# An attention kernel whose work order comes from a written-out table instead of per-beat patterns

## The chip, the cores and the metric

The kernel runs on one core of a Trainium2 chip. The metric is the device time of one execution in microseconds (us), the median of several runs. The program is one launch; every engine runs its own instruction stream, and semaphores order them.

## The reference

Eight images of 32 x 32 tokens with 128 channels pass through four attention layers in a row, all in fp32.

- Layers 0 and 1: group norm, then attention with 8 heads of 16 channels over the 1024 tokens of an image (softmax over 1024 keys), output projection, residual. 
- Layer 2: layer norm over the channels, attention with one head of 128 channels, projection, residual.
- Layer 3: group norm, attention with one head of 128 channels, projection, residual.

```python
def _L0_conv_ref(x, gn_scale, gn_bias, w_qkv, w_out, b_out):
    ...
    scores = jnp.einsum('bcq,bck->bqk', q, k) * hd ** (-0.5)
    scores = jax.nn.softmax(scores, axis=-1)
    o = jnp.einsum('bqk,bck->bqc', scores, v)
...
    x = _L0_conv_ref(x, ...)
    x = _L1_conv_ref(x, ...)
    x = _L2_conv_ref(x, ...)
    x = _L3_conv_ref(x, ...)
    return x
```

## The kernel before

**Work of a layer with heads (0 and 1).** An image and layer make a head stage of four rounds; a round is 4 heads by 512 queries. Per round TensorE makes

- 32 *tiles* (`score_tile`, L1292): scores of 128 queries by 512 keys for one head, contracted over one half of the array's rows (62 of 128); neighbouring tiles use opposite halves. VectorE takes the row maximum of each (L1084). A tile lands in one of `WORK_BANKS` = 3 PSUM banks, and the bank is free when VectorE has read it.
- one *shift* (L1278/L1280): the 16 columns of maxima are turned, split in two parts, and four DMAs put them into rows of `q_stack`, so that the second product of scores comes out with the maximum subtracted.
- 16 *pairs* (`pair`, L1320): scores again, keys by queries, with the shift in the product: two matmuls on opposite row halves into one of two PSUM buffers (`pairs`); ScalarE takes the exponential of 1024 columns (L973).
- 8 times *values* (`values`, L1346): the products of probabilities and values for 4 heads at once, each on 32 columns of the array, over 512 queries in one go (`("values", u, 0, 2)`) or in two halves of 256 (`("values", u, 0, 1)` and `("values", u, 1, 1)`).

So 64 rounds hold 2048 tiles, 1024 pairs and 512 slots; a *slot* is what lies between the values of one key block and those of the next: two pairs, one values, and as many tiles as the plan puts there.

**Work of a layer with one head (2 and 3).** For 128 queries at a time (`full` beats, 128 in all): *scores* (L1364), maximum on VectorE (L1116), exponential on ScalarE (L980), *turn* (eight transposes, L1208) and a copy by ScalarE (L989), and four steps *pv* per 128 queries (L1386). Seven phases of such beats are put between and behind the head stages.

**Chunks.** Everything else is a chunk: transposes of an image (`in`, `up`, `back`), the two group-norm products (`gn1`, `gn2`), the projections (`k0` to `v1`) and the output projections (`out0`, `out1`), of 512 columns each, all on TensorE with a bank of their own; and steps without a bank (`stats`, `apply`, `lnstats0`, `lnapply0` and so on). The text below calls the projections and output projections *products*. Where a product stands next to values it is issued as four matmuls of 32 columns (`by_columns`, L1217), else as one of 128 (L1214).

**What sets the order.** `Plan` writes one list, `plan.order`, when the program is built. Each engine walks the same list and issues its part of every item, so the list fixes the order on every engine and on the SP queue. `place_chunks` gives each chunk a beat. `place_tiles` spreads the tiles over the beats between what is available and what is due, as evenly in time as it can, where a head beat weighs 1.0 and a full beat `FULL_BEAT_WEIGHT` = 1.1. `beat(b)` then orders what a beat holds by a pattern chosen by its number of tiles (T a tile, P a pair, C the chunks of the beat, V values in one go, U one half of values):

```python
    PATTERNS = {0: "PCPV", 1: "TPCPV", 2: "TPCTPV", 3: "TPCTTPV", 4: "TPCTTPTV"}
    SHIFT_LAST = True
    HALVES_PATTERN = "TPTPCUTTV"
    CHUNK_PATTERNS = {0: "PPVC", 1: "TPPVC", 2: "TPTPVC", 3: "TPTPTVC", 4: "TPTCUTPTV"}
```

`count` walks the finished list and gives out banks, ring places and semaphore counts; a chunk in a beat with fewer than four tiles goes to a `work` bank (`narrow`), others to a `pairs` buffer. A wait in the list is thus bound to the item before it that used the same bank.

Of the kernel before, what the change touches and what calls it, by code (L numbers as in the profile page):

```python
# [1 line left out]

# [5 lines left out]
P = 128  # L8
# [16 lines left out]
SLOTS = KT * ROUNDS  # L25
# [32 lines left out]
HALVES = PROJECTIONS + ("out0", "out1")  # L58
# [13 lines left out]
class Plan:  # L72
# [5 lines left out]
    def __init__(self):  # L78
        self.beats, self.head_beat, self.full_beat = [], {}, {}
        n = 0  # L80
        for g in range(len(HEAD_STAGES)):
            for s in range(STAGE_SLOTS):
                self.head_beat[g, s] = len(self.beats)
                self.beats.append(("head", STAGE_SLOTS * g + s))
            for _ in range(KT * FULLS_AFTER.get(g, 0)):
                self.full_beat[n] = len(self.beats)
                self.beats.append(("full", n))
                n += 1
        self.full_tiles = n
# [58 lines left out]
    def place_chunks(self):  # L148
        h, f, put = self.h, self.f, self.put
        one = list(PROJECTIONS)  # L150
        two = ["k0+k1+q0+q1", "v0+v1"]
        ln = ["up", "lnstats0", "lnstats1", "lnapply0", "lnapply1", "back"]
        ln_fast = ["up", "lnstats0+lnstats1", "lnapply0+lnapply1", "back"]
        last = IMAGES - 1
        for i in range(IMAGES):
            g0, g1 = self.head_index[0, i], self.head_index[1, i]
            k2, k3 = self.full_index[2, i], self.full_index[3, i]

            if i == 1:
# [24 lines left out]
            if i < 2:  # L184
                end = self.chain(h(2 * i + 3, 6 if i == 0 else 1), 2, i, ln)
                self.project(end + 1, 2, i, one)
            elif i < last:
                end = self.chain(f(k2 - 1, 1), 2, i, ln_fast)
                self.project(h(2 * i + 3, 1), 2, i, one)
            else:  # L190
                self.project(self.chain(f(k2 - 1, 1), 2, i, ln_fast), 2, i, two)

            up = ["up", *NORM]
            if i < last - 2:
                at = h(6, 13) if i == 0 else h(2 * i + 6, 13)
                self.project(self.chain(at, 3, i, up), 3, i, one)
            elif i == last - 2:
                self.project(self.chain(h(15, 13), 3, i, up), 3, i, one)
            else:
                self.project(self.chain(f(k3 - 1, 1), 3, i, ["up", "stats", "gn1+gn2", "apply"]), 3, i, two)  # L200

    def place_tiles(self):


        ready = [0] * len(HEAD_STAGES)
        for g, b in self.available.items():
            slots = self.STACK_SLOTS
            while slots > 0:
                slots -= 1 if self.beats[b][0] == "head" else 2
                b += 1  # L210
            ready[g] = b
        tiles = [(r, n) for r in range(ROUNDS) for n in range(TILES)]
        ends = len(self.beats)
        time, most, least = [0.0], [self.FIRST_TILES], [self.FIRST_TILES]
        for b, (kind, _) in enumerate(self.beats):
            time.append(time[-1] + (1.0 if kind == "head" else self.FULL_BEAT_WEIGHT))
            most.append(TILES * ROUNDS_OF_STAGE * sum(r <= b for r in ready))
            least.append(0)
        for r in range(1, ROUNDS):
            due, slots = self.head_beat[r // ROUNDS_OF_STAGE, KT * (r % ROUNDS_OF_STAGE)], self.DUE_BEFORE  # L220
            while slots > 0 and due > 0:
                due -= 1
                slots -= 1.0 if self.beats[due][0] == "head" else self.FULL_BEAT_WEIGHT
            for b in range(max(due, ready[r // ROUNDS_OF_STAGE] + 5), ends + 1):
                least[b] = max(least[b], TILES * (r + 1))
        least = [min(low, high) for low, high in zip(least, most)]
        done, at = [float(self.FIRST_TILES)], 0
        while at < ends:
            low, high, low_at, high_at, to = -1.0, 1e9, at, at, at
            while to < ends and low <= high:  # L230
                to += 1
# [1252 lines left out]
```

## Time and profile before

| | |
|---|---|
| time, median of 3 runs | 2267.25 us (2265.59 to 2267.3) |
| span of the profiled execution | 2270.4 us |
| TensorE busy | 2160.2 us, 95% |
| VectorE busy | 1688.7 us, 74% |
| ScalarE busy | 1454.0 us, 64% |
| GpSimd busy | 408.0 us, 18% |
| mean granted TensorE clock | 0.983 |

The profiled execution's span is 2270.4 us, 3.1 us above the median of the runs; the profile's own time and the measured one can be taken as the same to 0.14%. A busy TensorE is not a TensorE at its peak: the end of a matmul in the profile is modelled, and where a matmul stands alone on one half of the array the engine counts as busy too. So the distance between the starts of neighbouring items says more than busy time.

### The profile page before, as it was taken

To read this page: it belongs to the slowest core of one execution; us is meant where nothing else is said; L and a number is where in the kernel's file an instruction comes from. 1 tells how busy PE (TensorE), PEld (TensorE's weight loads), DVE (VectorE), ACT (ScalarE), POOL (GpSimd) and SP (SyncE) were. 2 spreads that over 40 slices of the span, in tenths; PEclk is the share of its full clock that TensorE was granted. 3 is DMA by queue.
4 is the path that set the end of the run, shared out by engine and by line. 5 is a ranking of instruction groups with operands and counts; after the bars stand their busy time and mean duration, and the time that the engine had idled before them with its cause. 6 is when DMAs were issued, how large, how long until landed. Compare 5 with 4: busy or idle time off the path is not lost.

```text
span 2270.4 us, 41605 instructions
## 1 busy us (share of the span) xinstructions
PE 2160.2 (95%) x16748; PEld 1158.8 (51%) x16748; DVE 1688.7 (74%) x3104; ACT 1454.0 (64%) x1698; POOL 408.0 (18%) x541
## 2 busy tenths in 40 slices
PE   5999999999999999999999999999999989999999
PEld 3444344434643467434764347533574335745888
DVE  6899898889688876888668886788767956772433
ACT  1577677767477754778458774587646875476554
POOL 3102111220122311212111221203121030021231
PEclk7899999999999999999999999999999999999999
DMA  5403142230231403031130402204040050000000
GB/s 137 83 14 83 41 76 63 43 83 13 54 51 40 56 23 76 16 72 24 52 62 2 94 2 65 49 2 94 2 94 11 2 94 1 6 6 1 5 6 19
DMA packets 48590, 97.45 MB, mean 43 GB/s; under 512 B 7824, under 2 KB 10640, under 8 KB 48272
## 3 DMA queue, kind: packets, MB, share of 16 engines
q1 hardware_dynamic: 48400, 94.81, 20.1%
q8 instruction: 133, 2.18, 0.4%
q14 instruction: 57, 0.47, 0.1%
HBM read 55.98 MB, written 37.75 MB: 41 GB/s over the span
## 4 chain that ended last, share of the span: by engine, by line
PE 79%; DVE 13%; issue 4%; ACT 2%; POOL 1%; DMA 1%; SPq 0%; POOLq 0%; ACTq 0%; DVEq 0%
PE outs L1346 19%; PE work L1292 19%; PE outs L1386 11%; DVE part_max L1084 8%; PE pairs L1364 8%; PE pairs L1320 8%; PE pairs L1208 5%; PE work L1217 4%; PE pairs L1217 3%; PE work L1214 1%; DVE o_turn L1096 1%; DVE stats L1022 1%; DVE neg_max L1116 1%; ACT probs L973 1%; DMA q_stack<-shift_parts 1%
## 5 line engine op out<-in xcount | busy, mean ns | idle before, releaser
L1084 DVE TENSOR_REDUCE part_max<-work 128x1 f32<-128x512 f32 x2048 | 1284.5, 681 | 236.8 <-PE work L1292 232.2
L973 ACT ACTIVATE probs<-pairs 128x1024 f32<-128x1024 f32 x1024 | 1005.4, 1023 | 313.6 <-PE pairs L1320 298.6
L1292 PE MATMUL work<-k_stack,q_stack 62*128 62x512 f32 x2048 | 743.9, 468 | 31.5 <-DVE part_max L1084 20.7
L1320 PE MATMUL pairs<-q_stack,k_stack 64*128 64x512 f32 x2048 | 611.5, 440 | 13.4 <-DMA q_stack<-shift_parts 10.9
L1346 PE MATMUL outs<-probs,v_heads 128*32 128x256 f32 (+1 forms) x5448 | 584.2, 500 | 7.2 <-DVE o_turn L1096 6.9
L1292 PEld LDWEIGHTS work<-k_stack,q_stack 62*128 62x128 f32 x2048 | 317.2, 187 | 529.4 <-DVE part_max L1084 355.9
L1116 DVE TENSOR_REDUCE neg_max<-pairs 128x1 f32<-128x1024 f32 x128 | 156.6, 1223 | 236.2 <-PE pairs L1364 235.5
L1320 PEld LDWEIGHTS pairs<-q_stack,k_stack 64*128 64x128 f32 x2048 | 271.8, 186 | 57.1 <-ACT probs L973 31.0
L980 ACT ACTIVATE probs<-pairs,neg_max 128x1024 f32<-128x1024 f32 x128 | 142.8, 1115 | 245.9 <-DVE neg_max L1116 245.9
L1386 PE MATMUL outs<-v_full,probs 128*128 128x128 f32 x2048 | 258.6, 279 | 4.8 <-issue 4.8
L1386 PEld LDWEIGHTS outs<-v_full,probs 128*128 128x128 f32 x2048 | 242.5, 192 | 35.8 <-issue 32.1
L1346 PEld LDWEIGHTS outs<-probs,v_heads 128*32 128x32 f32 x5448 | 114.2, 108 | 222.7 <-issue 195.3
L1364 PE MATMUL pairs<-k_full,q_full 128*128 128x512 f32 x768 | 211.8, 411 | 7.2 <-ACT probs L980 2.5
L861 POOL TENSOR_TENSOR o_both<-o_turn,o_inv 128x256 f32<-128x256 f32 x64 | 39.7, 620 | 805.7 <-DVE o_inv L1099 805.6
L989 ACT COPY probs<-pairs 128x1024 f32<-128x1024 f32 x128 | 129.8, 1014 | 54.1 <-PE pairs L1208 54.1
L1364 PEld LDWEIGHTS pairs<-k_full,q_full 128*128 128x128 f32 x768 | 134.8, 188 | 53.9 <-issue 13.0
L1208 PE MATMUL pairs<-avg,probs 128*128 128x128 f32 x1024 | 134.3, 274 | 0.4
L1208 PEld LDWEIGHTS pairs<-avg,probs 128*128 128x128 f32 x1024 | 116.9, 142 | 19.8 <-issue 16.4
L883 POOL CAST parts<-parts 128x512 fp32r<-128x512 f32 x64 | 39.1, 611 | 270.8 <-ACT parts L944 270.5
L819 POOL TENSOR_TENSOR rstd<-var_eps,minus_half 128x1 f32<-128x1 f32 (+1 forms) x32 | 26.7, 834 | 328.5 <-DVE var_eps L1047 249.3
L885 POOL TENSOR_TENSOR parts<-parts 128x512 fp32r<-128x512 f32 x64 | 82.0, 1282 | 5.1
L1217 PE MATMUL work<-h,w 128*32 128x512 f32 x472 | 64.2, 602 | 0.0
(126 smaller groups left out, 1136.6 us busy)
## 6 DMA issues: line engine op xcount, KB each, us to landing
k_scratch<-parts SPq DMA_DIRECT2D x64, 256.0 KB
q_scratch<-parts SPq DMA_DIRECT2D x64, 256.0 KB
k_stack<-k_scratch SPq DMA_DIRECT2D x64, 256.0 KB, 7.0
q_stack<-q_scratch SPq DMA_DIRECT2D x64, 256.0 KB, 9.7
k_stack<-k_scratch SPq DMA_DIRECT2D x64, 128.0 KB, 8.3
q_stack<-q_scratch SPq DMA_DIRECT2D x64, 128.0 KB, 10.7
q_stack<-shift_parts SPq DMA_DIRECT2D x256, 4.0 KB
tmp<-x SPq DMA_DIRECT2D x7, 512.0 KB, 3.5
```

The costliest lines, as they stand in the source:

```text
L973: nc.scalar.activation(probs[:, plan.prob[u], 2 * n:2 * n + 2, :], pairs[:, plan.half["pair", t], :, :], ACT.Exp, scale=HEAD_SCALE).then_i ...
L980: nc.scalar.activation(p_full[:, n % 2, :], bank_of(("scores", n)), ACT.Exp, bias=neg_max1[:, n % SUMS:n % SUMS + 1], accum_out=sum1[:, n ...
L989: nc.scalar.copy(pT_full[m % 2][:, :, P * (n % 2):P * (n % 2 + 1)], bank_of(("turn", n)).rearrange("p (k q) -> p k q", q=P)).then_inc(f_co ...
L1084: nc.vector.tensor_reduce(part_max[:, r % 2, column:column + 1], bank_of(("tile", r, n)), AX_X, ALU.max, negate=True).then_inc(tile_max, 1)
L1116: nc.vector.tensor_reduce(neg_max1[:, n % SUMS:n % SUMS + 1], bank_of(("scores", n)), AX_X, ALU.max, negate=True).then_inc(f_max, 1)
L1208: last = nc.tensor.transpose(bank[:, P * n:P * (n + 1)], source(j), ident)
L1217: last = nc.tensor.matmul(to[some, :], weights[:, some], moving, start=True, stop=True)
L1292: nc.tensor.matmul(bank_of(("tile", r, n)), qs[rows, i, a, heads, P * t:P * (t + 1)], ks[rows, i, keys, heads, :], start=True, stop=True). ...
L1320: last = nc.tensor.matmul(pairs[:, plan.half["pair", t], half, :], ks[rows, i, key // QT, first + n, P * (key % QT):P * (key % QT + 1)], q ...
L1346: last = nc.tensor.matmul(outs[2 * HD * n:2 * HD * (n + 1), columns], v_heads[:, i, key, at:at + 2 * HD], probs[:, plan.prob[u], n, column ...
L1364: last = nc.tensor.matmul(pairs[:, plan.half["scores", n], half, :], q_full[:, k % 2, q, queries], k_full[:, k % 2, key, columns_of(half)] ...
L1386: last = nc.tensor.matmul(outs[:, P * j:P * (j + 1)], pT_full[m % 2][:, k, P * j:P * (j + 1)], v_full[:, at % 2, k, :], start=k == 0, stop ...
```

## The change

Three things change, all in `Plan`; no instruction of an engine is added or changed in kind.

1. The finished order goes through a new function, `arranged`. It takes tiles, pairs and all other items (class C) each from a queue of its own, in their old order, and merges them by a table of letters, `FIRST_STEPS` and `STEPS`. V and U make the values of the next slot, in one go or in halves. The patterns of `beat` still decide the order within class C, and nothing else.
2. The layer norm of the images 2 to 6 in layer 2 goes over six beats (`ln`) and not four (`ln_fast`).
3. In `place_tiles` a head beat with a product weighs 1.2 and not 1.0, so more tiles are given to such a beat. As the table fixes where tiles stand, this touches the place of the shifts among class C, and which products count as `narrow`.

```diff
@@ -100,7 +101,89 @@
             self.order += self.beat(b)
         m = self.full_tiles // 2 - 1
         self.order += self.full_values(2 * m + 1) + [("y", m)]
+        self.order = self.arranged(self.order)
         self.count()
+
+    FIRST_STEPS = "C" * 29 + "T" * 36 + "C" * 1 + "T" * 4
+    STEPS = (
+        "TPTPTTTPTCUTPTU TTPTCCUTPTU TTPTCCUTPTU TTPTCCUTPTU TTPTCCUTPTU CTPTCCUTPTU TTPTPCUTTU TPTPCCUTTU CTPTTPTV "
+        "TPTTPV TPTTPTV TPTPUTTU TPTPUTTU CTPTPTV TPTTUPTTU TTPPTTV CPPTTTUU PTTUTPTU TTPPTUTTU PPTTTV TTPPTV "
...
+        "CTTPUTTPU PCCTTCPTTCCV PTTTCCUTTPPTU CTTUCTPPTTU TTPCTUU CPPTTV PTTTPV TTPPTUTTU TPPTTV PTTTPV CPPTTTV "
...
+        "CCCTTTCCCCC CCTTCCTTCCCC CCCTTCCTTCCCC TTPCCTTTCCCCC CCTTPCCCCCCCCCTTTPCCCCPTTTCTCTTPCCTUCCPTTPU UU UTPPU "
...
+    )
+
+    def arranged(self, order):
+
+        queues = {n: deque(c for c in order if n == self.class_of(c)) for n in "TPC"}
+        slots = deque(range(SLOTS))
+        arranged, half = [], 0
+        for n in self.FIRST_STEPS + self.STEPS.replace(" ", ""):
+            if n == "V":
+                arranged.append(("values", slots.popleft(), 0, 2))
+            elif n == "U":
+                arranged.append(("values", slots[0], half, 1))
+                if half:
+                    slots.popleft()
+                half = 1 - half
+            else:
+                arranged.append(queues[n].popleft())
+        return arranged
+
+    def class_of(self, item):
+        return {"tile": "T", "pair": "P", "values": "V"}.get(item[0], "C")
@@ -185,7 +268,7 @@
             elif i < last:
-                end = self.chain(f(k2 - 1, 1), 2, i, ln_fast)
+                end = self.chain(f(k2 - 1, 1), 2, i, ln)
                 self.project(h(2 * i + 3, 1), 2, i, one)
@@ -213,7 +296,8 @@
         for b, (kind, _) in enumerate(self.beats):
-            time.append(time[-1] + (1.0 if kind == "head" else self.FULL_BEAT_WEIGHT))
+            chunk = any(c[0] == "chunk" and c[1] in HALVES for c in self.extra.get(b, []))
+            time.append(time[-1] + ((1.2 if chunk else 1.0) if kind == "head" else self.FULL_BEAT_WEIGHT))
```

## Rows read from the trace of the kernel before

**Rows 1.** The page, busy time of each engine over the span.

```profile
PE 2160.2 (95%) x16748; PEld 1158.8 (51%) x16748; DVE 1688.7 (74%) x3104; ACT 1454.0 (64%) x1698; POOL 408.0 (18%) x541
```

**Rows 2.** The page, chain that ended last, shares of the span by engine.

```profile
PE 79%; DVE 13%; issue 4%; ACT 2%; POOL 1%; DMA 1%; SPq 0%; POOLq 0%; ACTq 0%; DVEq 0%
```

**Rows 3.** Waits over the whole span: waiter, releaser, total us, times, longest us.

```profile
PEld work L1292 <- DVE part_max L1084: 355.9, 638, 1.7
```

**Rows 4.** Timeline of TensorE, slots of three tiles: start, length, instructions.

```profile
932.52 1.07 PE L1346 MATMUL outs<-probs,v_heads 128*32 128x512 f32 x8
933.51 0.49 PE L1292 MATMUL work<-k_stack,q_stack 62*128 62x512 f32 x1
...
934.63 1.07 PE L1346 MATMUL outs<-probs,v_heads 128*32 128x512 f32 x8
```

**Rows 5.** Timeline of VectorE in the next slot.

```profile
934.04 1.89 DVE L1084 TENSOR_REDUCE part_max<-work 128x1 f32<-128x512 f32 x3 [0.22 <-PE work L1292]
```

**Rows 6.** Timeline of ScalarE in the slot after that.

```profile
936.46 1.94 ACT L973 ACTIVATE probs<-pairs 128x1024 f32<-128x1024 f32 x2 [0.18 <-PE pairs L1320]
```

**Rows 7.** Timeline of TensorE, values in halves, four tiles a slot.

```profile
119.98 0.64 PE L1346 MATMUL outs<-probs,v_heads 128*32 128x256 f32 x8
...
120.97 0.64 PE L1346 MATMUL outs<-probs,v_heads 128*32 128x256 f32 x8
...
123.48 0.64 PE L1346 MATMUL outs<-probs,v_heads 128*32 128x256 f32 x8
```

**Rows 8.** Timeline of TensorE, a slot of four tiles, values in one go.

```profile
963.81 1.06 PE L1346 MATMUL outs<-probs,v_heads 128*32 128x512 f32 x8
...
966.50 0.64 PE L1346 MATMUL outs<-probs,v_heads 128*32 128x512 f32 x4
```

**Rows 9.** Timeline of TensorE, a product and three tiles in a slot.

```profile
914.45 1.06 PE L1346 MATMUL outs<-probs,v_heads 128*32 128x512 f32 x8
915.33 1.04 PE L1217 MATMUL work<-h,w 128*32 128x512 f32 x8
916.30 0.50 PE L1292 MATMUL work<-k_stack,q_stack 62*128 62x512 f32 x1
...
917.62 0.64 PE L1346 MATMUL outs<-probs,v_heads 128*32 128x512 f32 x4
```

**Rows 10.** Timeline of TensorE, a product and four tiles in a slot.

```profile
199.98 0.64 PE L1346 MATMUL outs<-probs,v_heads 128*32 128x256 f32 x8
...
203.31 0.42 PE L1346 MATMUL outs<-probs,v_heads 128*32 128x256 f32 x4
```

**Rows 11.** Windows: three slots without a product, then five with one each.

```profile
932.52:938.88 6.36, 6.36 (x47) 2.48 (x46) 5.67 (x10) 4.71 (x6) 0.00 (x0) 1.00 0.01 3
911.07:927.15 16.08, 16.04 (x166) 6.83 (x165) 10.27 (x18) 13.18 (x17) 5.79 (x7) 1.00 0.11 35
```

**Rows 12.** Timeline, all engines, the slot behind a group norm's statistics.

```profile
946.73 1.29 DVE L1022 BATCH_NORM_STATS2 stats<-x 128x6 f32<-128x512 f32 x2
...
947.18 1.07 PE L1346 MATMUL outs<-probs,v_heads 128*32 128x512 f32 x8
...
950.49 0.64 PE L1346 MATMUL outs<-probs,v_heads 128*32 128x512 f32 x4
```

**Rows 13.** Timeline of TensorE in a full phase, a lone tile.

```profile
831.67 0.49 PE L1292 MATMUL work<-k_stack,q_stack 62*128 62x512 f32 x1
832.09 1.13 PE L1214 MATMUL work<-h,w 128*128 128x512 f32 x2
```

**Rows 14.** Timeline of TensorE, the pair that waits for shift 59.

```profile
1873.79 1.22 PE L1320 MATMUL pairs<-q_stack,k_stack 64*128 64x512 f32 x4 [9.16 <-DMA q_stack<-shift_parts]
```

**Rows 15.** Timeline of TensorE, slots without tiles, near the end.

```profile
2064.72 1.06 PE L1346 MATMUL outs<-probs,v_heads 128*32 128x512 f32 x8
...
2066.66 0.51 PE L1320 MATMUL pairs<-q_stack,k_stack 64*128 64x512 f32 x2 [0.42 <-ACT probs L973]
2067.09 1.06 PE L1346 MATMUL outs<-probs,v_heads 128*32 128x512 f32 x8
```

More of the change, by code:

```diff
@@ L1 @@
+from collections import deque
 from contextlib import ExitStack
@@ L102, in __init__ @@
         self.order += self.full_values(2 * m + 1) + [("y", m)]
+        self.order = self.arranged(self.order)
         self.count()
+    FIRST_STEPS = "C" * 29 + "T" * 36 + "C" * 1 + "T" * 4
+    STEPS = (
+        "TPTPTTTPTCUTPTU TTPTCCUTPTU TTPTCCUTPTU TTPTCCUTPTU TTPTCCUTPTU CTPTCCUTPTU TTPTPCUTTU TPTPCCUTTU CTPTTPTV "
+        "TPTTPV TPTTPTV TPTPUTTU TPTPUTTU CTPTPTV TPTTUPTTU TTPPTTV CPPTTTUU PTTUTPTU TTPPTUTTU PPTTTV TTPPTV "
+        "TCTPPTTTV TTPPTUTTU TPPTTV CTTPTPUU TTUTPPTTU TTPTPCV TTTPCTTPV TTPPTV TCPTPTTV TPTPTUTTTU TPPTTUU CTTPPTV "
+        "TPTTPTV TTPTTPV CTTTCUTPTTPCU TTPPV CTPTTUCPTPTTU CUTPCTTU TPPTV CTPTTCUPTTPU TTCPTTV TTPTCCCUTTPTU "
+        "CTTPUTTPU PCCTTCPTTCCV PTTTCCUTTPPTU CTTUCTPPTTU TTPCTUU CPPTTV PTTTPV TTPPTUTTU TPPTTV PTTTPV CPPTTTV "
+        "PTTPV TTTV CCTTTPTPPTTCPV TTTPPV TTTPCV CTTPTTPTCTPTTV PTPTTV TCPTTPTUU CTCPPTTUTTU TTPPTUTTPU PCTTTCV "
+        "TPTTCPTTUPTTU UTTCPTU CCCTTPTCUPTTU CTTCCCPTTCV TTPTCTTPTCUTCPTPU TPCTV PPTTUU CCCPTPTTV CTPPTTUTTPTU "
+        "TPTUCTPPTTU TPTV TPCTTUCU TPTTUPTTU TTPTUTPTU TTTPPTV PCTTTPUU PTPTTV TPTPTV TPTTUPTPTU TTPUTTU CTPPTTUTTU "
+        "TTPPTV TTTPPV CTPTTPV TTPTUTTPTU TTPCPTV PTTCTTTPV PTPTTV CTPPTTTV TPTTPV TTTPPV CPTTTCPTTV PTTTCUCPTTPU "
+        "TTCTCTCPV TTTPUCCTTPTCCU TPTTV CTPPTTTCCTTCCPCTTUPCTCPU V TCPTTPV PCTPTTTPCPTTPTUU CCV TTTPPV CTTUTTPPTU "
+        "TTCTPTTV PTTCCCTPTTV TPTUTPTU TTPCTTPTV PCTTCUTPTTCTPTCU TTPPTV TTTPV TPPTTV PTTTPV CTPPTTTUTPTU "
+        "TTCTTPTPTTPV V PPCCTTTV TPPTUTTTPPTTU CCV TTPTCCUTPTU PTTUPTTU CPTTPTV TPTTUTCPTU TTPPTV CPTTCPTTV "
+        "PTTTCUTTPU CPTTCTTCPCV TTTPUCCTTPU CTTPUTTCPTTCCCCTTTPPTTPTU CCUU TPTV CTPPTTV CCTTPTPUU TTPPTV "
+        "CTTTPPUCTPTTU TPPTTUU CPTTTV CTPPTTV TTTUPTTPTU TPPTTV CTPTTPUU PTPTTV TPPTTUTPTTU TPPTTV TTPTV CTPPTTTPTV "
+        "TTPTV TPPTTV CTPTTPV PTTPTV CTTPPTV PTTUPTTPU TTCPTTTV PPTTV PTTTPV CCV CCTTC CTTCCC TTTCCCCTTCC CCCCTTTCC "
+        "CCCTTTCCCCC CCTTCCTTCCCC CCCTTCCTTCCCC TTPCCTTTCCCCC CCTTPCCCCCCCCCTTTPCCCCPTTTCTCTTPCCTUCCPTTPU UU UTPPU "
+        "TPTTCV PPTTTUU PTTPV CTTTPCPTTV TPTTUPTTCU CPTTCPTTV CPTTPUTTU CPTTTUCPTTU PTTUPTTCU TTPTCTTPTV PPTCTV "
+        "PTTTPV TPTPV PCTTTPV PTTCCTPTTUTTPPTU V CTTPPTV PTTUCPTPTTU TPTV CPTTUTPTU TPTPTV CCTTPTPUTPU PTTTV CTPTPTV "
+        "PCTTTPUCPTTTU TPPTV TTPTV TTPPTV TTPTPV CTTPTCUTPTU PTTCUTPTPU TCTCPTTCCCV PTTUCTPTTCU PCTTUPTTPU "
+        "TTCCCCCTTPV PCTTTPCV TTPPTCUU CTTPPTV CPTPTTV CTPTPTTV TTTPPTV PTTCCTTTPPCCV PTTV PTTPTV TPPTTUU CCPTTPV "
+        "TTPTPUCTPTTPU CTTPTV TPTTV PTPTTV CPTPTUTTPU CCPTTTV PPTTCCTTV PCPTTTV CTPTCTTTPV PPCTTV TTPTCPTTV PPTTTV "
+        "PTTPV PTTTPV CCV CCTTTC CTCCC TTTCCCTTCCC CCCCCC CCCTTCCTTCCC CCTTTCCCCCC CCCTTTCCCCCC CCTTCCTTCCCC "
+        "CCCTTTCCCCCCC CCTTTCCCCC CCCCCCTTCCCC TTTCCTTCCCCCCC CCTTTCCCCCC CCCTTCCCC TCTTCCCCTTCCC PTTCCCCTTCC "
+        "CTTTPCCCCTTCCTTPCCCCPTTV PTTTPV CTPPTUTTCCU PTTCPTTTV PPTTV TTPCUPTTTCU PTTPV TTPTPUU CTPPTTV TPCPTTV "
+        "TTPTPUU PTTTPV PTPTTV CPTPTV TTPTCTPTCUU PTTPV CPTTPTUU TPPTV CTPTPTTV CTCPTTPV PTTTPV TPPTTUU PTTTPV "
+        "CTPPTTV CPTPTTUU TPPTTV TPTTPTV PCTTTPV TTPPCV TPPTTV TPTTPV PTTTPV CCPTTUPTTU CPPTTTV CTTCPCCCTTTV "
+        "PTTPCCPTTV TPTCTCCV TTPCCTTTPPV CPTTTCPV CPTPCTUU CPTTPCUU PTTTPV CPTPTTV CPTTPTV TPTPV TTTPCTPTV PCCTTPV "
+        "TPTPTUU CPTTPTV CPTPTTV CPTPTTCV PTTPTV TPPTTV CPTTPUCTPTCU TTTV PPTTCCPTTTV CPTPTCV TTPTCCTTPV PPTTV "
+        "TTPTCTPTV PPTTTV PTTPV PTTTPV CCV CCTTTC CTCCTTC CCCCCC CCTTTCCCC CCCTTCCTTCCC CCCTTTCCCCC CCCCTTTCCCCC "
+        "CCTTCCTTCCCC CCCTTTCCCCCCC CCCTTTCCCC CTTTCCCCCCCTTCC CCCCTTCCCCC CCTTTCCCCCC CCCTTCCCC CTTTCCCCTTCCC "
+        "PTTTCCCCCTC CPTTCCCCCCTTTPCCCCTTUTPPTU TTPTV CCTTPPUTTCPTTU CTTPTV TPPTCV PTTCTTPTV PTTPTV PTTPV CPTTCTPUU "
+        "TTPPTV TPTTPUU PTTTPV CTPPTV TTPTCTTPCV PTPTTV TPPTV PCTTTPUU TPPTTV CTPPTTV CTPTTPV TPCTTPV TTPTPV PTTTPV "
+        "TTPPTTUCU CPTPTV TTPTPV CPTTTPV PTTV TTPCPTTPV TPTTPV TPTTPV TTPTPV CCTTPUPTTCU PPTTTV TPTCCCCCPTTTV "
+        "PPTTCCPTTCCV TPPTTV TPCTTCCTTUTPPTCU V CTCPTTPV CCPTPTTV PPTTUU CCPTPTTV CPTPTTV TPTPV TTPTCTTPV PPCCTTTUU "
+        "TPPTUU PCTTTPV CPTPTTV CCTPPTTV PTTTPV TPTPTV CCTPTCTTPV PPTTTV CTPTCTTPV CPPTTTV CPTTCUTPTPTU TPCTV "
+        "PTPTUTTCU TTPTPV TPTTPUU PTTTPV CCV CCTC CTTTCCC TTTCCTTCCCC CCCCCC CTTTCCCCTTCCC CCCCTTCCCC CCCTTTCCCCCC "
+        "CCTTCCTTCCCC CCCCTTTCCCCCC CCTTCCTTCCC CCCCCCCCCTTC CCTTCCTTCCCCC CCTTTCCCCCC CCTTCCCCC TCTTCCTTCCCCC "
+        "TTPCCCCCTC CTTPTCCCCCCTTTPCCCCTTUTPTPU TTPTV CCTTPPUTTU CPTTTCUPTTPCU PPTTTV UPTTTCU TPPTTV TTPTPV CPCTTPTV "
+        "PTTPTV TPPTTV PTTTPV CPTTPTV TPTPTV PTTTCTPTV CPTPV PCTTTPV TPPTTV CPTTTPV CTPCPTTV TTPTPV TTPTPUU PTTTPV "
+        "CTPPTTUU CPTTTPV PTPTTV PCTTTPV TPPTTCV TPPTTV TTPTPV TPTTPV TPTTPV CCTTPUPTTCU TPPTTV TTPCCCCCTPTTV "
+        "TPPTCCTPTV CTTTPCTTCPTCCCCV PTTTPV PTTV CPCTTPV PCTTTPV PTTPV CPTTTPV CTPPTTV CPTTTCCTPTV CPTTPTUU PTPTV "
+        "TPTV PPCCTTTPV TPPTTV CTPTTPV PCTTTPV TPPTTV CPTTUCTPTU CPTTTV PTTPCPTTCV CPPTTTV CTPTCCTTTPV TPPTV "
+        "TPTTCPTTV PPTTV PTTTPV TPTPV CCV CCTTTC CTCCC TTTCCCCCC CCCTTTCCC CCCTTCCTTCCC CCCTTTCCCCC CCCTTTCCCCCC "
+        "CCTTTCCCCCC CTTCCTTTCCCCCCC CCCCTTTCCC CCCTTCCCCCCC TTCCCCCCCCC TCTCCCTTTCCCC CCTTCCCCC CCCCCTTTCCC "
+        "TPTTCCCCCTTC CTTPTCCCCCCPTTTCCTPTCCTTPV PTTTPV CCTPTUTTU CTTPTV PPTTCCTPTTV TPTPCV TPTTPV TPTTPV CTTPPTV "
+        "PTPTTV TPPTTV PTTTPV CTPPTTV PTTTPV TTPPTV TPTTPV PCTTTPV PTTPTV TTPPTV TPTTPV TPTTPV TTPTPV PTTTPV CTPPTTV "
+        "PCTTTPV PTTPCV TTTPPV TTPTCTTPV TTPPTV PTTTPV TPPTTV TTPPTV CTPPTTV CPPTTTV TPPTTV PCTTTPV CPPTTTV TPTPUU "
+        "CTTTPPUU TPTUU PPCTTCTPTTV CTPPCTV PTTTUCTPTTU TPPTV CCCCPTTTUCTTPU TPTUTTPPTCU CCCCUPTTTPU CCCTPTV PCPCTTV "
+        "PTTTPCV CTPPTCTV PTTCCTPV PTPV CCPPV CPPV CPTPTV CCCPPTTV TPTTPV CPPTTV CTPTTPV CPPTTV PTTTPV PTTPV CV "
+        "CCTTC CTTCCC TTTCCCCCC CCCTTTCCC CCCTTCCTTCC CCCCCTTCC CCTTTCCCCC CCTTTCCCC CCCTTTCCCC CCTTCCCC "
+        "CCCCTTTCCCTTC CCCTTCCCC CCTTTCCCCCC CCCCTTTCCC CCTTTCCCCCC PTTCCCCCTTC PCTTCCCCCCCTPTCCCCTTPPV TTCTPTTV "
+        "PTPTTV PTPTTV CTPPTCCV TTTPCUPTTPU TTPV TPPTTV CPTTPV TTPPTV CPTTPV PTTTPV TPTPV TTTPCTTPV CPTPTTV PTPTUU "
+        "CCPTTPV TPTTPV CPTTTCPV PTTTPUU PPV CCPPCV PPCV PPV CCPPCV PPUU PCPPV PUCPU PCPPV V PPV CV CCC CCCC CCCCCC "
+        "CCCCCC CCCCCCC CCCCCC CCCCCCC CCCCCC CCCCCCC CCCCCC CCCCCCCC CCCCCCCC CCCCCCCCC CCCCCCC CCCCCCCCCCC "
+        "CCCCCCCC CCCCCCC CCCCCC CCCCCCCC CCCCCCC CCCCCCCCC CCCCCCC CCCCCCCCCCC CCCCCCCC CCCCCCC CCCCCC CCCCCCCC "
+        "CCCCCCC CCCCCCCCC CCCCCCC CCCCCCCCCCC CCCCCCCC CCCCCCC CCCCCC CCCCCCC CCCCCC CCCCCCC CCCCCC CCCCCCC CCCCC "
+        "CCCCCCCCCC "
+    )
```

## The prediction

> **What bounds the kernel now.** I read the page first: TensorE is busy for 95% of the span and holds 79% of the chain that ended last, VectorE 13% of it [rows 1, 2]. That looks like a plain TensorE bound, under which an order could gain nothing. The waits say otherwise: before 638 tiles the weight load waited for VectorE to give a bank back, 355.9 us together [rows 3]; much of it lies under a running matmul. So I went to the timelines, and measured from the start of one values to the start of the next.
>
> A slot of three tiles lasts 934.63 - 932.52 = 2.11 us: 0.99 us for the values and 1.12 us for three tiles and two pairs [rows 4]. These are seven matmuls on half the array, so four passes of two; a lone tile, one pass, costs 832.09 - 831.67 = 0.42 us [rows 13]. A pass is therefore (1.12 - 0.42)/3 = 0.23 us and each run of tiles and pairs has 0.19 us besides. An odd count wastes half a pass. In the same slot VectorE needs 1.89 us for three maxima, 0.63 each [rows 5], ScalarE 1.94 us for two exponentials [rows 6]. So three engines stand within 10% of each other, and TensorE leads by little.
>
> With four tiles it is VectorE that leads: 4 x 0.63 = 2.52 us, and a slot with the values in halves lasts 123.48 - 120.97 = 2.51 us [rows 7]; with the values in one go it lasts 2.69 us [rows 8], since the fourth tile asks for a bank too early. Behind a group norm's statistics (1.29 us on VectorE) the same four tiles last 3.31 us [rows 12]. Beside a product it is the reverse: product, three tiles and values last 3.17 us [rows 9], and VectorE is busy for 10.27 of 16.08 us (64%), against 5.67 of 6.36 (89%) in slots without one [rows 11]. Four tiles beside a product cost 3.33 us [rows 10], so the fourth costs 0.16 us there, and 0.40 to 0.58 us elsewhere. The old patterns put three tiles into both kinds of slot. That is what an order can change.
>
> How much there is: leaving out the first 20 slots and those with full beats, 479 slots remain, which last 1365 us together in the trace. For each I took the largest of three demands at the prices above (TensorE: 0.19 a run, 0.23 a pass, 0.9 a product, 0.9 or 2 x 0.47 for values; VectorE 0.63 a tile and its other operations; ScalarE 0.97 a pair and its other operations). Their sum is 1315 us; taking the demands over two neighbouring slots, so that a burst may be made up next door, it is 1288 us. So about 77 us over those slots is time in which the leading engine waited; some 10 us of it is one wait for a shift's DMA [rows 14].
>
> **The change, part by part.** The letters can be counted from the diff, with class C in the order of the kernel before (the new weight shifts a few shifts in it).
>
> *Tiles moved between slots.* Slots with a product and no burst on VectorE had 3.15 tiles on average and get 4.09; slots with neither had 3.32 and get 2.98. VectorE's demand in the latter falls from 2.16 to 1.94 us, below TensorE's 2.05, which leaves it room to catch up behind a burst. Summed as above, the table's order gives 1309 us slot by slot and 1270 over two neighbours: -18 us against before. Passes are counted in it: in the head stages they rise, as more runs are odd. Bounds: -6 (slot by slot) and -18. I take -18, since three banks let TensorE run ahead by about a slot.
>
> *Values in one go.* 169 slots had halves, 140 have; a half is 0.57 us at most, being 0.99 of [rows 7] less the run of two tiles (0.42), so two halves cost 1.14 against 0.99: 29 x 0.15 = -4 us, already in the sum above.
>
> *Runs of four tiles or more* fall from 55 to 28. Each costs 2.69 - 2.51 = 0.18 us beyond VectorE's own demand [rows 7, 8]: -5 us. Bounds: 0 to 27 x (2.69 - 2.11) = -16.
>
> *Full phases.* Before the last one, tiles stood as RFTTTppppT, a lone tile costing as much as two. The six phases with tiles have 255 passes and 141 runs before, 221 passes and 139 runs after: 34 x 0.23 + 2 x 0.19 = -8 us. Bounds: 0, if scores or turns are what is waited for, and -9. The seventh phase has no tiles or pairs, and its letters are all C: nothing changes there.
>
> *Order within a slot.* Before, the product stood first and VectorE ran dry behind values and product; then three tiles came at once. The table puts tiles on both sides of it (CTPPTTTUTPTU). Pairs stand together or at the ends (TTPPTTV, PTTTPV), which no slot with tiles had before. Of the 77 us of waits 49 are left when the DMA's 10 and the moved tiles' 18 are taken off. I take -14, under a third of it; bounds: -49, and on the other side +37 (below).
>
> *Layer norm over six beats.* Five images; two steps each are split. A burst next to tiles costs 3.31 - 2.69 = 0.62 us [rows 8, 12], so ten at most are worth -6 us; in full beats VectorE has few tiles and I take 0. `back` comes two beats later, and the projections of that image wait in head stage 2i+3, stages away. Nothing on the SP queue moves for it.
>
> *The weight of 1.2* gives more tiles to product beats, but the table has the last word on tiles. What is left is where shifts stand, and that fewer products are `narrow` and go into a pairs buffer; a product in `work` costs 3.17 and one in `pairs` 3.33 with a tile more [rows 9, 10]. Taken as 0, bounds 3 us either way.
>
> *What stays.* The first 70 items are as they were, and so is the start. Pair 944 still follows shift 59 by two slots and two products, so its 9.16 us for the DMA [rows 14] stay; likewise the slots without tiles at the end [rows 15]. Writes, reads and shifts keep their order on the SP queue.
>
> Sum: -18 - 5 - 8 - 14 = -45 us. From the profiled execution's 2270.4 us that is 2225; its distance to the median, 3.1 us, taken off: **2222 us**, 2.0% less than 2267.25.
>
> The Trainium skill, "TensorEngine Tiling (Array Packing)", section "Key Properties", says that a change of the tiling mode drains the engine. Here values that are followed by a product in columns cost 915.33 - 914.45 = 0.88 us, by a tile 0.99 [rows 4, 9], so the trace agrees with 0.11 us a switch. By that rule alone the change is worth its 18 fewer runs, two switches each: 4 us.
>
> **Rivals.**
>
> *Pairs side by side wait for ScalarE (slower).* Two pair buffers serve all pairs, and a pair needs the exponential before last. Slots of two adjacent pairs without tiles last 2067.09 - 2064.72 = 2.37 us though TensorE needs 0.99 + 0.66 and ScalarE 1.94; one pair waited 0.42 us for ScalarE [rows 6, 15]. The table has 153 slots with tiles and adjacent pairs, where there was none. If each loses 2.37 - 2.11 = 0.26 us or more, that is +40 us; with the moved tiles' gains then falling away in those slots, and the full phases' -8 and the runs' -5 kept, some +12 to +20 remain: 2283 us. It decides from 0.3 us a slot on, the 45 us spread over 153. For it: rows 15. Against: only 41 times do two such slots follow each other; often a slot like PTTTP stands between, which spaces the pairs out.
>
> *VectorE stays the bound (small gain).* If the bunches of three tiles and slots of five and six with a product meet VectorE's 0.63 a tile, no burst is caught up: then only -6, -8 and a few us, -15 us: 2252 us. The waits of [rows 3] speak for it. The Trainium skill has this as a rule, same page, section "PSUM Bottleneck": tiling makes TensorE faster but not the reading out of PSUM, which may become the bound. In slots of four tiles the trace agrees (2.51 against 4 x 0.63).
>
> *The order recovers most waits.* If the table was laid out so that each item stands where its inputs are ready, most of the 77 us less the DMA's 10 go, and further time in the first twenty slots and full phases: -80 us or more, 2183 us.
>
> *It does nothing.* TensorE's work is the same to 1%, and gains in one slot are taken back by another engine in the next, as all three stand within 10%: 2267 us.
>
> **How the numbers follow.** Forecast (-20 to -75 us) 0.57; most waits recovered 0.09; small gain 0.14; nothing 0.06; pairs against ScalarE 0.14. Faster by over 0.2% (4.5 us, about what a measurement tells from no change): 0.80; within: 0.06; slower: 0.14. The range leaves out the far part of the first and the last case: 2180 to 2274. The forecast's own range is 2192 to 2247.
>
> **What would show it.** Right: waits of the weight loads for VectorE well under 355.9 us; VectorE's busy share evener between slots with and without a product; the stretch of a full phase some 1.5 us shorter in each of the middle four; the wait of pair 944 still near 9 us. Wrong: waits of pairs L1320 for ScalarE (adjacent pairs) of tens of us; values waiting for exponentials; slots with five tiles above 3.8 us; a shift whose DMA is waited for at another place, as a tile queue that runs later makes the maxima late.

## The result and the profile after

The changed kernel takes 2160.8 us (median; 2154.8 to 2161.75) against 2267.28 us before: a ratio of 0.9521, 95% interval 0.9508 to 0.9533, 106 us less. In three of the experiments (e4, e6, e11) one execution took two to three times as long as the others; the ratios leave it out. The forecast was 2222 us with a range of 2180 to 2274, so the direction was right; the time lies outside the range, and the gain is more than twice the one forecast.

The page after: span, busy times, then the chain that ended last by engine.

```profile
span 2158.1 us, 39609 instructions
...
PE 2096.4 (97%) x15750; PEld 1168.3 (54%) x15750; DVE 1687.8 (78%) x3104; ACT 1447.0 (67%) x1698; POOL 408.0 (19%) x541
...
PE 84%; DVE 8%; DMA 2%; issue 2%; ACT 2%; POOL 1%; SPq 1%; POOLq 0%; DVEq 0%; ACTq 0%
```

VectorE and ScalarE work as long as before [rows 1]; VectorE's share of the chain falls from 13% to 8% [rows 2]. The waits over the span (waiter, releaser, us, times, longest):

```profile
PEld work L1376 <- DVE part_max L1168: 233.0, 443, 1.2
...
PEld pairs L1404 <- ACT probs L1057: 128.8, 244, 0.9
...
PEld pairs L1404 <- DMA q_stack<-shift_parts: 17.0, 7, 9.5
```

Waits of tiles for VectorE fell from 355.9 to 233.0 us [rows 3]; waits of pairs for ScalarE rose, from 31.0 us in the trace of before to 128.8. Nearly all of that is a wait of the weight load; the matmuls of pairs themselves stood idle for ScalarE for 0.7 us in all.

A busy share can't say where 106 us went, so I summed start-to-start distances of TensorE's items by kind. "Runs" are unbroken sequences of tiles and pairs, "priced" is what they should take at the prediction's 0.19 us a run and 0.23 a pass; the rest of a run is counted as waiting. The tail (the last phase with full beats) has no tiles. Head and full work are mixed where a phase ends, so the split between them depends on where the cut is put, by some 5 us.

```
us                        before   changed   table alone
start, to first pairs       69.8      69.8        69.8
head stages               1516.5    1437.9      1465.3
  of these, runs           748.2     678.6       703.4
  runs, priced             601.3     611.1       611.1
full phases                482.2     448.0       471.6
  of these, runs            84.1      62.9        67.4
tail                       193.8     193.8       193.8
```

The head stages give 79 us, the full phases 34 (31 if a phase is taken from its first *scores* to its last *pv* step). In the head stages the priced work of the runs rose by 10 us and their waiting fell from 147 to 68 us.

A slot of three tiles is what it was: 2.12 us from values to values, against 2.11 [rows 4].

```profile
1166.23 1.06 PE L1430 MATMUL outs<-probs,v_heads 128*32 128x512 f32 x8
...
1168.35 1.06 PE L1430 MATMUL outs<-probs,v_heads 128*32 128x512 f32 x8
```

The windows show where the difference lies: four slots without a product, then six slots with four products, then a whole full phase; the last line is the same phase in the kernel before.

```profile
1176.00:1183.63 7.63, 7.52 (x62) 2.88 (x54) 7.21 (x14) 6.46 (x9) 0.62 (x1) 1.00 0.01 2
1242.00:1260.50 18.50, 18.50 (x135) 7.36 (x136) 14.63 (x28) 15.77 (x19) 8.12 (x14) 1.00 0.01 2
1023.10:1105.10 82.00, 81.39 (x514) 64.07 (x513) 58.58 (x119) 38.74 (x56) 9.86 (x10) 1.00 0.31 69
```

```profile
1077.70:1166.20 88.50, 84.90 (x530) 64.56 (x526) 60.84 (x125) 40.16 (x57) 12.22 (x11) 1.00 0.30 64
```

VectorE is busy for 14.63 of 18.50 us (79%) in the second window. The 64% of [rows 11] were measured with a product in each of five slots, here two of the six slots hold two each, so the two aren't the same work. Taken over all slots with a product from the 21st on, without those with full beats, VectorE is busy for 78% of the time in the changed kernel and was for 67% before; in slots without a product it is 92% and was 90%. The full phase shown is 6.5 us shorter.

TensorE's granted clock stood at its lower level, 1.2 GHz, for 27 us of the execution before (the first 70 us left out) and for 14 us after; the rest of the time it was 2.4 GHz. At half speed that is 7 us of difference at the most, so the clock can't be more than a small part of the 106 us.

### The profile page after: what moved, and what is told of

The parts are those of the page before. It is cut to its first block, busy times and chain, and to the rows that moved or that the text cites. A ratio compares the mean times of both kernels' runs of the same rounds, so it can differ in the third digit from the quotient of the medians.

```text
span 2158.1 us, 39609 instructions
## 1 busy us (share of the span) xinstructions
PE 2096.4 (97%) x15750; PEld 1168.3 (54%) x15750; DVE 1687.8 (78%) x3104; ACT 1447.0 (67%) x1698; POOL 408.0 (19%) x541
## 4 chain that ended last, share of the span: by engine, by line
PE 84%; DVE 8%; DMA 2%; issue 2%; ACT 2%; POOL 1%; SPq 1%; POOLq 0%; DVEq 0%; ACTq 0%
PE outs L1430 21%; PE work L1376 17%; PE pairs L1404 12%; PE outs L1470 11%; PE pairs L1448 8%; DVE part_max L1168 6%; PE pairs L1292 6%; PE pairs L1298 3%; PE pairs L1301 2%; PE work L1298 2%; DMA q_stack<-shift_parts 2%; PE work L1301 2%; ACT probs L1057 1%; DVE neg_max L1200 1%; SPq L853 1%
## 5 line engine op out<-in xcount | busy, mean ns | idle before, releaser
L1376 PE MATMUL work<-k_stack,q_stack 62*128 62x512 f32 x2048 | 609.7, 453 | 5.9 <-DVE part_max L1168 3.8
L1430 PE MATMUL outs<-probs,v_heads 128*32 128x512 f32 (+1 forms) x5216 | 565.8, 512 | 0.8 <-DVE o_turn L1180 0.2
L1404 PE MATMUL pairs<-q_stack,k_stack 64*128 64x512 f32 x2048 | 509.0, 446 | 15.4 <-DMA q_stack<-shift_parts 14.0
L1376 PEld LDWEIGHTS work<-k_stack,q_stack 62*128 62x128 f32 x2048 | 286.9, 187 | 316.3 <-DVE part_max L1168 233.0
L1404 PEld LDWEIGHTS pairs<-q_stack,k_stack 64*128 64x128 f32 x2048 | 224.9, 185 | 220.1 <-ACT probs L1057 128.8
L1470 PEld LDWEIGHTS outs<-v_full,probs 128*128 128x128 f32 x2048 | 250.8, 191 | 37.3 <-issue 28.8
L1470 PE MATMUL outs<-v_full,probs 128*128 128x128 f32 x2048 | 269.7, 279 | 0.2
L1180 DVE STREAM_TRANSPOSE o_turn<-outs 128x512 f32<-128x512 f32 x64 | 45.3, 708 | 9.5 <-PE outs L1430 9.5
```

Source lines behind the costliest of these rows:

```text
L1376: nc.tensor.matmul(bank_of(("tile", r, n)), qs[rows, i, a, heads, P * t:P * (t + 1)], ks[rows, i, keys, heads, :], start=True, stop=True). ...
L1404: last = nc.tensor.matmul(pairs[:, plan.half["pair", t], half, :], ks[rows, i, key // QT, first + n, P * (key % QT):P * (key % QT + 1)], q ...
L1430: last = nc.tensor.matmul(outs[2 * HD * n:2 * HD * (n + 1), columns], v_heads[:, i, key, at:at + 2 * HD], probs[:, plan.prob[u], n, column ...
L1470: last = nc.tensor.matmul(outs[:, P * j:P * (j + 1)], pT_full[m % 2][:, k, P * j:P * (j + 1)], v_full[:, at % 2, k, :], start=k == 0, stop ...
```

## The experiments

"Ratio" is to the kernel before, run on the same chip. Three questions: which part of the change, which property of the table, and what makes order cost time.

### Which part

**e1: without the table.**

```diff
-        self.order = self.arranged(self.order)
```

> The table is left out; the layer norm over six beats and the weight of 1.2 stay, and the old patterns order each beat. If the gain of 106 us comes from the table (where items stand), this stays at 2267 us, or falls to some 2255 as the weight gives product beats a fourth tile for 0.16 us each. If these two side changes carry it (products in a pairs buffer, no burst of two layer-norm steps), it falls by tens of us, to under 2230.

2253.1 us, ratio 0.9945 (0.9926 to 0.9965). The two traces differ by 18.6 us. The six full phases are 14 us shorter, with the old patterns. Head stage 14, up to the next full phase, is 8.5 us shorter; the wait of pair 944 for the DMA lies there, 9.2 us before and at most 2.7 here. The other head stages together are a little longer.

**e2: the table alone.**

```diff
-                end = self.chain(f(k2 - 1, 1), 2, i, ln)
+                end = self.chain(f(k2 - 1, 1), 2, i, ln_fast)
...
-            time.append(time[-1] + ((1.2 if chunk else 1.0) if kind == "head" else self.FULL_BEAT_WEIGHT))
+            time.append(time[-1] + ((1.0 if chunk else 1.0) if kind == "head" else self.FULL_BEAT_WEIGHT))
```

> The table alone, with the four-beat layer norm and weight 1.0 of the kernel before. If the table carries the gain, 2161 us within 5. If the side changes carry part, it is above 2175.

2207.8 us, ratio 0.9741 (0.9725 to 0.9758). The table alone is worth 58 us; the side changes, 13 us without it, are worth 47 with it. Both of my alternatives for e1 and e2 had assumed that parts add up.

**e5 and e6: the table with one side change each** (one of the two lines of e2's diff each).

> Table and weight 1.2, layer norm over four beats. The table alone gave 2208 us, with both side changes 2161. If the weight brings the 47 us (it takes 46 products out of the work banks and moves ten shifts), this is near 2165 us. If the layer norm brings it, near 2205 us.

2180.2 us, ratio 0.9619 (0.9595 to 0.9643): the weight brings 28 us. Its head stages take 1442.1 us against 1465.3.

> Table and layer norm over six beats, weight 1.0. If the weight brings the 47 us, near 2203 us; if the layer norm does, near 2165 us. Both near 2185 us would say that they share it.

2192.5 us, ratio 0.9667 (0.9644 to 0.9690): the layer norm brings 15 us. Its full phases take 452.4 us against 471.6, its head stages are as in e2.

**e7 and e8: banks alone.** The weight decides which products are `narrow` (155 chunks before, 109 after). Here that set is computed with the other weight, and the order is the same item by item.

```diff
         self.shifted = set()
+        placed = self.place_tiles(1.0)
         self.narrow = {c for b, (kind, _) in enumerate(self.beats)
-                       if kind == "full" or len(self.tiles.get(b, [])) < 4 for c
+                       if kind == "full" or len(placed.get(b, [])) < 4 for c
```

> The changed kernel with its order kept item by item; only the 46 products that the weight moved from the three work banks to the pairs buffers go back to a work bank. If the banks are what the weight is worth, it loses most of what the kernel without the weight loses: 30 us or more, over 2190 us. If the places of the shifts and of the chunks are, it stays within 5 us of 2161.

2172.5 us, ratio 0.9576 (0.9551 to 0.9601): 12 us slower than the changed kernel.

> The counterpart: the table alone (2208 us), order kept item by item, but those 46 products in pairs buffers as in the changed kernel. Banks: 2180 us or less. Places of shifts or the layer norm: within 5 us of 2208.

2194.2 us, ratio 0.9679 (0.9653 to 0.9706): 14 us faster than e2. So 12 to 14 of the weight's 28 us are 46 products that no longer take one of three work banks from the tiles. Neither alternative was wholly right; the other half lies in the places of shifts and chunks, which I didn't take apart.

### Which property of the table

**e3: the table's counts, the old order in each slot**; for example `TTPTCTTPCV` becomes `TTPTCCUTPTU`.

> The changed kernel with the number of tiles, pairs and chunks in each slot kept as in its table, but each slot's letters (from the seventh slot on, slots with full beats left as they are) put in the order of the old patterns: products first or in the middle, TPTTPV, TPTPUTTU. If it matters in which slot a tile stands (tiles beside products), most of the gain stays, 2180 us. If it matters where in the slot items stand, most of the head stages' 78 us are lost and only the full phases' 34 stay: 2235 us.

2282.9 us, ratio 1.0075 (1.0059 to 1.0091): slower than before, by 122 us slower than the changed kernel. The full phases, left as in the table, keep all of their gain (448.0 us). Not all of the rest is waiting. TensorE's granted clock stood at 1.2 GHz for 75 us of this execution, 48 us of it before 560 us, against 14 us in the changed kernel. This run, the changed kernel and the kernel before, from 70 to 560 us; the third value from the end is the granted clock:

```profile
70.00:560.00 490.00, 455.50 (x3717) 189.04 (x3717) 404.64 (x719) 313.65 (x346) 74.34 (x107) 0.95 0.28 57
```

```profile
70.00:560.00 490.00, 482.23 (x3781) 216.39 (x3782) 456.34 (x814) 354.99 (x395) 76.35 (x110) 0.99 0.29 58
```

```profile
70.00:560.00 490.00, 468.13 (x4460) 198.14 (x4460) 438.06 (x779) 344.36 (x376) 75.69 (x109) 0.99 0.28 58
```

If TensorE lost half of its speed in all of that time, the clock accounts for (75 - 14)/2 = 31 of the 122 us. That is my estimate of its most; 91 us or more are waiting and longer slots. The order also changes which slots have their values in halves (163 against 140).

**e4: the old counts, the table's order in each slot.**

> The counterpart: number of tiles in each slot as in the kernel before, full beats as before, no side changes, but each slot's letters taken from the nearest slot of the table with as many tiles, pairs and products. If placement within the slot carries the head stages' gain: 2267 - 60 = 2205 us or less. If the distribution over slots carries it: above 2245 us.

2286.6 us, ratio 1.0091 (1.0071 to 1.0111). So in these two trials neither the distribution nor the style of order was worth anything alone. Both theories fall in the form in which I put them; an order fits only the counts that it was made for.

From here on the changed kernel is the base, and one property is taken away at a time.

**e10: products first**, in 102 slots; `TTPTCTTPCV` becomes `CTTPTTTPCV`.

> The changed kernel; in 102 slots the product (with the chunks in front of it) goes to the head of the slot, directly behind the values, as the old patterns had it. If tiles on both sides of a product are what keeps VectorE fed, each such slot loses 0.2 to 0.4 us: 2180 to 2200 us. If the order of tiles and pairs carries the 128 us between this kernel and the one with old patterns in each slot, it stays below 2170.

2241.6 us, ratio 0.9888 (0.9871 to 0.9905): 81 us slower, 0.8 us a slot and twice my upper estimate. Slot by slot, the 102 changed ones are 77 us longer in the trace and the 404 others 4. One of them in both traces, TensorE and then VectorE. The changed kernel:

```profile
1229.87 1.06 PE L1430 MATMUL outs<-probs,v_heads 128*32 128x512 f32 x8
1230.87 0.50 PE L1376 MATMUL work<-k_stack,q_stack 62*128 62x512 f32 x2
1231.20 0.40 PE L1404 MATMUL pairs<-q_stack,k_stack 64*128 64x512 f32 x2
1231.44 0.40 PE L1376 MATMUL work<-k_stack,q_stack 62*128 62x512 f32 x1
1231.79 1.09 PE L1292 MATMUL pairs<-avg,y 128*128 128x128 f32 x8
1232.81 0.50 PE L1376 MATMUL work<-k_stack,q_stack 62*128 62x512 f32 x2
...
1233.48 0.64 PE L1430 MATMUL outs<-probs,v_heads 128*32 128x512 f32 x4
```

```profile
1231.40 2.64 DVE L1168 TENSOR_REDUCE part_max<-work 128x1 f32<-128x512 f32 x4 [0.61 <-PE work L1376]
```

With the chunk (here the transposes `up`) first:

```profile
1288.48 1.07 PE L1421 MATMUL outs<-probs,v_heads 128*32 128x512 f32 x8
1289.49 1.09 PE L1283 MATMUL pairs<-avg,y 128*128 128x128 f32 x8
1290.51 0.50 PE L1367 MATMUL work<-k_stack,q_stack 62*128 62x512 f32 x2
...
1291.08 0.40 PE L1367 MATMUL work<-k_stack,q_stack 62*128 62x512 f32 x1
1291.79 1.09 PE L1367 MATMUL work<-k_stack,q_stack 62*128 62x512 f32 x2 [0.31 <-DVE part_max L1159]
...
1293.05 0.64 PE L1421 MATMUL outs<-probs,v_heads 128*32 128x512 f32 x4
```

```profile
1291.05 2.48 DVE L1159 TENSOR_REDUCE part_max<-work 128x1 f32<-128x512 f32 x4 [1.64 <-PE work L1367]
```

The same five tiles and one chunk take 3.61 us with the chunk in the middle and 4.57 in front. In front, VectorE idles 1.64 us behind values and chunk, then gets five tiles in a row, and the fourth and fifth wait for banks. In the middle it idles 0.61 us, and works off the first three tiles under the chunk. The granted clock stood at 1.2 GHz for 24 us in this execution, so at most 5 of the 81 us are the clock, by the same estimate.

**e11: the old alternation of tiles and pairs** in 408 slots (`PTTTPV` becomes `TPTTPV`), chunks and values in place.

> The changed kernel; places of chunks and values kept, but tiles and pairs take their places in the old alternation (TPTTP, TPTPTT) in 408 slots. If the order of tiles against pairs matters most: over 2220 us. If the products' places do: under 2185.

2241.2 us, ratio 0.9881 (0.9859 to 0.9902): 80 us slower, of which the clock (31 us at 1.2 GHz) is at most 9. Both halves of e3 count, and they don't add up either (81 + 80 against 122).

**e9: adjacent pairs taken apart** in 142 slots (`TPPTTV` becomes `TPTPTV`).

> The changed kernel; in 142 slots in which two pairs stand side by side and a tile is next to them, one pair and that tile change places (TPPTT to TPTPT). The waits of pairs for ScalarE rose from 31 to 129 us. If they cost time, as the prediction's slower rival has it, this is faster than 2161 by 10 us or more. If they lie under a running matmul and the table's pairs stand where the buffers are free, it is the same within 5 or slower.

2161.8 us, ratio 0.9538 (0.9523 to 0.9552), the changed kernel's time. Pairs side by side are neither harm nor gain. But the waits stayed too:

```profile
PEld pairs L1395 <- ACT probs L1048: 125.2, 235, 0.8
```

125.2 us against 128.8. So it isn't the neighbouring pairs that make them, and this run doesn't show what they cost. It shows something else: 142 slots can be rearranged at no price, so the 80 us of e10 and e11 aren't what any disturbance of the table costs.

**e12: values in one go** in 131 slots (`TTPPTTUCU` becomes `TTPPTTCV`).

> The changed kernel with the values in one go in the 131 slots that have halves: 131 x 0.15 = 20 us less work by the prediction's price. If the halves are there to give VectorE time between tiles, the runs get longer and wait: 2170 us or more. If not, 2141 us.

2178.6 us, ratio 0.9612 (0.9596 to 0.9629): 18 us slower. Items of values took 11 us less in the head stages, runs 29 us more. In the trace the 131 slots themselves got 14 us shorter and the 375 others 37 us longer: the time is paid next door. That VectorE is still behind there is my reading; it wasn't tested.

### What makes order cost time

**e13, e14, e15: half maxima.** The maximum is taken over 256 of a tile's 512 keys.

```diff
-                                            bank_of(("tile", r, n)),
+                                            bank_of(("tile", r, n))[:, 0:HALF // 2],
```

> The kernel before, but VectorE takes a tile's maximum over 256 of its 512 columns only (the softmax is then shifted by another value), 0.3 us a tile less. If the 106 us are time in which TensorE waited for VectorE to free a bank, the old order no longer loses it: 2140 us within 20. If they are TensorE's or ScalarE's own, it stays near 2250.

2188.0 us, ratio 0.9643 (0.9621 to 0.9665): 80 us less than the kernel before, not the 127 that I had put. Most of the waits of tiles stayed:

```profile
PEld work L1292 <- DVE part_max L1084: 255.9, 459, 1.6
```

355.9 us became 255.9: 100 us less of waits for 80 us less of time. The granted clock was at 1.2 GHz for 24 us less than in the kernel before, which is 12 of the 80 at the most.

> The changed kernel with the same half maximum. Banks: the gap to the old order with half maximum closes from 106 to under 30 us, and this one gains less than the old order does, 2115 us. Otherwise the gap stays near 100 us.

2138.5 us, ratio 0.9424 (0.9404 to 0.9444): 22 us less than the changed kernel.

> The changed kernel with products at the head of 102 slots (80 us slower than the changed kernel with full maxima), with the half maximum. If the product in the middle is worth 80 us because it gives VectorE time between tiles, nearly nothing is left of the 80: within 15 us of the changed kernel with half maxima. If the product's place costs TensorE or ScalarE something itself, 40 us or more are left.

2161.9 us, ratio 0.9530 (0.9516 to 0.9544): 80 us less than e10.

The gap between old and new order closes from 106 to 50 us, that of the product's place from 81 to 23. So 44 to 56 of the 106 us and 53 to 58 of the 81 (the lower ends with the clock taken off) hang on how long VectorE takes for a maximum, and with it on when a bank comes free. The rest isn't shown to be something else: a bank is still held for matmul and half a maximum, and in e14 the weight loads of tiles still wait 179.0 us for VectorE.

**e16 and e18: shift 59 ahead of the reads.** Both kernels wait at pair 944 for the DMAs of shift 59 [rows 14]; after:

```profile
1774.95 0.79 PE L1404 MATMUL pairs<-q_stack,k_stack 64*128 64x512 f32 x2 [8.60 <-DMA q_stack<-shift_parts]
```

```diff
+        arranged.remove(("shift", 59))
+        arranged.insert(arranged.index(("read", 15, "k0")), ("shift", 59))
         return arranged
```

and in the table 14 tiles of the slots 463 to 468 moved to 14 of the slots 445 to 462.

> An attempt to better the changed kernel: in its trace pair 944 waits 9.6 us for the DMAs of shift 59, which stand in the queues behind the 16 transfers that read the stacks of stage 15. Fourteen tiles of round 59 go one each into the slots 445 to 462, and shift 59 goes ahead of those reads. The wait goes, 14 slots get a fourth tile (0.1 to 0.4 us each) and six lose theirs: 2155 us. If the wait comes from the shift's own way and not from the transfers ahead of it, 2165.

2157.4 us, ratio 0.9513 (0.9493 to 0.9534). The waits of pairs for a shift fall from 17.0 to 5.0 us:

```profile
PEld pairs L1399 <- DMA q_stack<-shift_parts: 5.0, 4, 2.2
```

This run alone doesn't prove that the transfers ahead were the cause: it also leaves 16.7 us between the issue of the shift and pair 944, against 13.7. The landings do. The last of the 16 reads lands at 1774.07 us in the changed kernel and pair 944 starts 0.9 us later; before, it is 1872.77 and 1.0 us; in e1, where the shift is issued 8.0 us ahead of the pair, it is 1860.89 and 0.9 us. In all three the pair goes right behind the last read, however long ago the shift was issued. Runs in the head stages took 6 us more. Whether it is a gain was tried once more, beside the changed kernel on one chip:

> The changed kernel once more, beside the next one on the same chip: 2161 us, ratio 0.952.

2158.0 us, ratio 0.9517 (0.9500 to 0.9534).

> The version with shift 59 ahead of the reads once more. If the 3.5 us by which it was ahead are real, its ratio is 0.0015 under the changed kernel's; if not, the two agree.

2160.7 us, ratio 0.9529 (0.9513 to 0.9545). The two agree: what the wait gave went into slots with a tile more. No version with whole maxima beat the changed kernel.

## Why the prediction was wrong, point by point

**Order within a slot: mis-sized, the main failure.** The term was -14 us, "under a third" of the waits left, and nothing stood behind the third. The failed step is this share. In the 479 slots that the prediction reckoned with, the time went from 1365 to 1291 us while the two-neighbour sum of demands went from 1288 to 1270. So the waits went from 77 to 21 us, and some 9 us of either are the wait of pair 944: nearly all that was open was recovered, 56 us. With the table alone the slots take 1320 us, 27 us of waits recovered, twice the term; the side changes made room for the rest. A slip made it worse. The 18 us of moved tiles were taken off the waits ("49 are left"), though moving tiles lowers the sum of demands and uses up no wait; 67 us were open.

The demands themselves were a fair floor only over two slots: the changed kernel comes in below its slot-by-slot sum (1291 against 1309), but not below the two-neighbour one (1270). In the runs the waiting fell from 147 to 68 us. And with the counts of the changed kernel, order alone makes 122 us of difference (e3, at most 31 of them the clock).

**Tiles moved between slots: wrong as a term of its own.** It had -18 us. The counts with the old order are 17 us slower than before (e3). A tile beside a product is cheap, as [rows 9, 10] say, only if the product stands so that VectorE works under it; e10 shows the same five tiles at 3.61 and at 4.57 us.

**Values in one go, -4 us: the sign was right, the use wrong.** Whole values do take less, 11 us over 131 slots in e12, 0.08 us a slot where the price was 0.15; but the kernel becomes 18 us slower. **Runs of four tiles, -5 us:** no run tests this term by itself.

**Full phases, -8 us.** The table alone gives 482.2 - 471.6 = 11 us, near the term; by other cuts of a phase it is 8 us (first *scores* to last *pv* step) to 15 (to the first values behind it). The 34 us of the whole change lie beyond its bound of -9, because the side changes act there.

**Layer norm, "I take 0", at most -6; weight, "taken as 0, bounds 3 us either way".** They brought 15 and 28 us with the table. For the weight, 12 to 14 us are the banks (e7, e8): I had compared two slots [rows 9, 10] and not asked how often a product in a work bank leaves the tiles two. For the layer norm the full phases shortened by 19 us (e6), and "in full beats VectorE has few tiles and I take 0" was the wrong step: in e1, without the table, they shorten by 14 us too, of which some 4 are fewer passes and runs there. How much of the 19 us with the table is the evener load on VectorE stays open: the letters C take items by count, so another number of steps per beat also moves 80 pv steps and 20 turns to other letters than the table was made for.

**What stays: right.** Start, tail, a slot of three tiles, and the wait of pair 944 (9.16 us before, 8.60 after).

**The rivals.** Pairs side by side: waits for ScalarE did rise (31.0 to 128.8 us), as its sign had it, but they stay at 125.2 when the neighbouring pairs are taken apart, so the mechanism named isn't what makes them (e9). "VectorE stays the bound": not at its 2252 us, though even the changed kernel gains 22 us when VectorE's maxima are halved (e14). "The order recovers most waits", given 0.09, came nearest: it named 2183 us for a table "laid out so that each item stands where its inputs are ready". Its signs were in the letters: pairs staggered over neighbouring slots, five and six tiles where a product parts them. I read those as unevenness to be priced.

The sum missed by 61 us. With the side changes at zero it was a forecast for the table alone, and there -45 stands against -58; the other 47 us were put at nothing. That -45 came as near as this is in part luck: of its terms the moved tiles have no value of their own, and the order was worth twice its -14 already.

## What to carry to other kernels

Where three engines stand within 10% of each other, take the whole gap between the measured time of a stretch and the engines' demands as open to a better order, and give a reason for any smaller share; and sum the demands over at least two slots, since one slot's largest demand isn't a floor when buffers let the engines run out of step. Put long work of the leading engine that needs nothing from the lagging one between the items that do, not in front of them. A written-out order fits one set of counts and bank places: after changing either, lay it out anew, and don't add up parts that were measured apart.

## What the runs showed of the hardware

**Small DMAs behind large ones.** Four small DMAs of 4 KB each, issued at 1761.25 us in the trace of the changed kernel, let pair 944 go at 1774.95, 13.7 us later, behind 16 reads of 128 and 256 KB issued from 1748.42 us on, the last of which landed at 1774.07. Issued ahead of those reads, no wait for a shift was longer than 2.2 us.

**A wait can bring the clock down.** In the changed kernel TensorE waits 8.60 us for that shift; the granted clock falls from 2.4 to 1.2 GHz at 1769.0 us, within the wait, and is back at 1779.2, 4.2 us after pair 944 went. The pair's two matmuls show 0.79 us, against 0.40 in the slot at 1231.20. So this wait costs more than its own length. The sum of waits doesn't tell how much clock is lost: in e3 it was at 1.2 GHz for 75 us with 347.0 us of waits of tiles for VectorE, in the kernel before for 27 us with 355.9. What brought it down in e3 wasn't traced.

**The wait of a weight load is no measure of lost time.** Before tiles the weight load waited 355.9 us for VectorE, but the matmuls of tiles themselves stood idle for it for 20.7 us. From before to after these waits fell by 122.9 us and the time by 106; with half maxima they fell by 100.0 us and the time by 80 in the old order, and by 54.0 us (233.0 to 179.0) and 22 in the new. So a wait of a weight load is neither free nor lost in full, and only a run with less of it shows what it is worth.
